# A four-stage transformer kernel on one core: row and column tiles of TensorE for the first cross attention

## What is computed

```python
x = x + tanh(g_xattn[0]) * L0_xattn(layernorm(x), ctx_1024, ...)   # stage A
x = x + tanh(g_ffn[0])   * L0_ffn(layernorm(x), ...)               # stage B
x = x + tanh(g_xattn[1]) * L1_xattn(layernorm(x), ctx_1024, ...)   # stage C
x = x + tanh(g_ffn[1])   * L1_ffn(layernorm(x), ...)               # stage D
```

```python
q = _ln((x @ Wq + bq).reshape(b, s1, H, HD), qn_w, qn_b)
k = _ln(kv[..., :HD], kn_w, kn_b)            # main; k_dca in the same way
ctx = _attn(qT, k, v)                        # softmax(q k^T / 4) v, per head
ctx_dca = _attn(qT, k_dca, v_dca)
return (ctx + ctx_dca) @ Wo + bo
```

## Time and profile before

| what | us |
|---|---|
| median of 3 runs (458.19 to 460.11) | 458.24 |
| the profiled execution, its own time | 458.89 |
| its span, first to last instruction | 457.1 |
| start to the first scores of stage A (TensorE at 30.74) | 30.7 |
| stage A from there to the first matmul of stage B (131.62) | 100.9 |
| stages B, C and D | 325.5 |

### The profile page before, as it was taken

How to read it: one execution, slowest core, us unless ns; L and a number is a source line. 1 busy time by engine, 2 the same in 40 slices (tenths; PEclk the granted TensorE clock), 3 DMA queues, 4 the chain that set the end, 5 groups by cost and what they waited for, 6 DMA issues and landing times. The chain is left out here.

```text
span 457.1 us, 8007 instructions
## 1 busy us (share of the span) xinstructions
PE 413.4 (90%) x3098; PEld 385.6 (84%) x3098; DVE 326.3 (71%) x727; ACT 206.9 (45%) x420; POOL 164.6 (36%) x199
## 2 busy tenths in 40 slices
PE   1877898987999999998989999999999999699995
PEld 1656887876889999997979899999998989599994
DVE  4787738686248696867755889889989979946642
ACT  4376347575323333243433654556456255323331
POOL 4115214242302213132222544754653553433332
PEclk9999589999899999999999999999999999989999
DMA  7201202020300110303010001001000100000000
GB/s 229 86 17 54 70 1 69 1 69 1 115 3 1 61 55 2 115 1 116 2 43 29 1 1 60 2 1 50 11 1 2 48 1 2 0 1 24 25 24 24
DMA packets 6811, 16.27 MB, mean 36 GB/s; under 512 B 1123, under 2 KB 4452, under 8 KB 6261
## 3 DMA queue, kind: packets, MB, share of 16 engines
q1 hardware_dynamic: 6772, 15.75, 10.3%
HBM read 14.70 MB, written 1.05 MB: 34 GB/s over the span
## 5 line engine op out<-in xcount | busy, mean ns | idle before, releaser
L1514 POOL TENSOR_SCALAR work<-work,lut_step,lut 128x344 f32<-128x344 int32 (+1 forms) x60 | 42.1, 713 | 55.6 <-DVE work L1441 53.7
L308 PE MATMUL ps<-wB_hi,workr 128*128 128x256 f32 x224 | 51.9, 295 | 6.1 <-POOL workr L1669 4.6
L308 PE MATMUL ps<-xT_hi,wB_hi 128*128 128x256 f32 x176 | 51.7, 293 | 0.0
L308 PE MATMUL ps<-xT_hi,wB_lo 128*128 128x256 f32 x176 | 50.1, 284 | 0.0
L308 PE MATMUL ps<-xT_lo,wB_hi 128*128 128x256 f32 x176 | 50.1, 284 | 0.0
L308 PE MATMUL ps<-wN_hi,shared_r 128*128 128x256 f32 x256 | 47.5, 280 | 1.2 <-DVE x L1428 1.2
L1107 POOL TENSOR_TENSOR workr<-work,workr 128x256 fp32r<-128x256 f32 (+1 forms) x36 | 22.9, 636 | 69.8 <-ACT workr L990 69.8
L308 PEld LDWEIGHTS ps<-wB_hi,workr 128*128 128x128 f32 x224 | 38.9, 191 | 8.1 <-POOL wB_lo L1519 3.8
L1456 DVE COPY_PREDICATED work<-work 128x1376 f32<-128x1376 int32 (+5 forms) x36 | 41.3, 1147 | 2.3
L308 PEld LDWEIGHTS ps<-wN_hi,shared_r 128*128 128x128 f32 x256 | 40.1, 188 | 1.5 <-DVE shared_r L1418 1.3
L308 PE MATMUL ps<-xT_hi,wM_hi 128*128 128x256 f32 x128 | 36.7, 287 | 3.6 <-ACT work L1282 2.2
(11 more groups left out here) (209 smaller groups left out, 1179.2 us busy)
## 6 DMA issues: line engine op xcount, KB each, us to landing
stage<-in_wC SPq DMA_DIRECT2D x4, 1280.0 KB, 5.5
stage<-in_wB SPq DMA_DIRECT2D x4, 768.0 KB, 4.3
stage<-in_idx SPq DMA_DIRECT2D x4, 536.0 KB, 3.4
stage<-in_wA SPq DMA_DIRECT2D x2, 512.0 KB, 5.4
out<-x SPq DMA_DIRECT2D x4, 256.0 KB, 2.1
x<-in_x SPq DMA_DIRECT2D x2, 256.0 KB, 4.9
x<-in_x SPq DMA_DIRECT2D x1, 512.0 KB, 6.2
ctx_n<-in_ctx_n SPq DMA_DIRECT2D x4, 128.0 KB, 2.1
```

The lines of the kernel that those rows point to most:

```text
L308: last = nc.tensor.matmul(out, l, r, start=start and i == 0, stop=stop and i == 2)
L1514: nc.gpsimd.tensor_scalar(lev[:, j, 0:n], bits[:, 0, 0:n], lut_step[:, j:j + 1], lut[:, 2 * j:2 * j + 1], ALU.mult, ALU.add).then_inc(*C[" ...
```

## The change

Scores: the keys stay undivided in `kT`; each head pair has a 32-row tile of `qx` and of `kT`, four such tiles (rows 0, 32, 64, 96) work for four banks. 32 matmuls of 64 columns take the place of 8 of 256. Values: the weight operand is now `v2`, 32 columns (two heads, of which one is zero), the moving operand 64 columns of `pT`; tiles are 64 rows by 32 columns, and the output has features in its rows, so `an`, its four copies and its turn are gone. 64 matmuls take the place of 16. The softmax halves are head pairs (banks 0 and 1, then 2 and 3), each over all four sequences, and one semaphore stands behind all the scores. The four `an` copies and `act_A_k` leave ScalarE, and `dve_A_k` has two instructions for six. `pe_A_values` waits for both halves' `pT`.

Biases: `bias_sel` adds the upper and the lower part in one matmul for two (both stand in `bias_r`, rows 0 to 63 and 64 to 127). `pe_A` is put in another order, `an_lo` is waited for between the two shifts, and the `keep_warm` counts differ: none between values and scores, 12 and 4 in the last group. `wS_lo` and the mask setup move from the start and group 0 to the end of group 2; the `sel` copies from ScalarE to GpSimd; `wS` and `sel` load beside `stage`, not into it. At the start, the lower parts of `wA` are made in three pieces, the output weights' last.

```diff
-        def pe_A_scores(pe, n, t):
+        def pe_A_scores(pe, n):
...
             for c in range(DC):
-                o = ps[:, 2 * t + c, :].rearrange("p (a b n) -> p a b n", a=PAIRS0, b=2)
-                for b in range(2):
-                    k = c * BG + 2 * t + b
-                    last = nc.tensor.matmul(o[:, :, b, :], qx[:, k].rearrange("p h n -> p (h n)"),
-                                            kx[:, k], start=b == 0, stop=False,
-                                            skip_group_check=True)
+                for b in range(BG):
+                    k = c * BG + b
+                    for p in range(PAIRS0):
+                        r = slice(32 * p, 32 * p + 32)
+                        last = nc.tensor.matmul(ps[:, p, k * S:(k + 1) * S], qx[r, k].rearrange("p h n -> p (h n)"),
+                                                kT[r, k], start=k == 0, stop=False, skip_group_check=True)
             last.then_inc(*A["scores_done"].up())
...
-        def pe_A_values(pe, g, t):
...
-            for k in range(8):
-                last = nc.tensor.matmul(ps[:, VALUES + 2 * t, k * 64:(k + 1) * 64], pT[:, t, k, :],
-                                        vz2[g % 2][:, t, k].rearrange("p b n -> p (b n)"), start=True, stop=True)
...
+            for i in range(DC * TILES):
+                for h in range(2):
+                    for p in range(PAIRS0):
+                        for b in range(2):
+                            r = slice(S * b, S * b + S)
+                            last = nc.tensor.matmul(ps[32 * p:32 * p + 32, VALUES + 2 * b, i * S:(i + 1) * S],
+                                                    v2[g % 2][r, i % TILES, i // TILES * PAIRS0 + p, h],
+                                                    pT[r, p // 2, p % 2 * 4 + i, h * S:(h + 1) * S],
+                                                    start=i == 0 and h == 0, stop=h == 1, skip_group_check=True)
+            last.then_inc(*A["pv_done"].up())
...
             if more:
                 pe_A_kv_main(pe, n, 0)
+            pe_A_shift(pe, g, 0)
+            if more:
+                pe.wait_ge(*A["an_lo"].at(g, 0))
                 pe_A_kv_last(pe, 0)
                 pe_A_kv_bias(pe, 0)
-            pe_A_shift(pe, g, 0)
-            if g:
-                pe_A_turn_out(pe, g - 1)
-            if more:
+            pe_A_shift(pe, g, 1)
+            if more:
+                pe_A_q_main(pe, n)
+                pe_A_q_bias(pe)
                 pe_A_kv_main(pe, n, 1)
-            pe_A_shift(pe, g, 1)
-            if more:
                 pe_A_kv_last(pe, 1)
                 pe_A_kv_bias(pe, 1)
...
         def pe_A_end(pe):
-            keep_warm(6, 0)
-            pe_A_turn_out(pe, GROUPS - 1)
-            keep_warm(5, 0)
+            keep_warm(8, 0)
             pe_A_out(pe, GROUPS - 1)
             keep_warm(9, 0)
```

More of the change, by code:

```diff
@@ L319, in build @@
         pT = take(TILES * 1024).rearrange("p (t k n) -> p t k n", t=TILES, n=P)
-        vz2 = [take(TILES * 8 * 2 * 32).rearrange("p (t k b n) -> p t k b n", t=TILES, k=8, b=2) for _ in range(2)]
+        v2 = [take(TILES * 8 * 2 * 32).rearrange("p (t k h n) -> p t k h n", t=TILES, k=8, h=2) for _ in range(2)]
         bias = take(NVEC + NVK)
-        vec, veck = bias[:, 0:NVEC], bias[:, NVEC:]
-        bq, bkv = vec[:, 0:D], veck
+        b_q, b_out = slice(0, D), slice(3 * D, 4 * D)
+        b_kv = slice(D, 3 * D)
         offset = take(TILES)
@@ L362, in pe_A_kv_bias @@
         def pe_A_kv_bias(pe, t):
-            for b in (bias_hi, bias_lo):
-                last = nc.tensor.matmul(kv_bank(t), ident_A, b[:, NVEC:], start=False, stop=b is bias_lo)
-            last.then_inc(*A["kv_done"].up())
+            nc.tensor.matmul(kv_bank(t), bias_sel, bias_r[:, b_kv], start=False, stop=True
+                             ).then_inc(*A["kv_done"].up())
         def rows_by_weights(to, l_hi, l_lo, r_hi, r_lo):
@@ L376, in rows_bias @@
         def rows_bias(to, cols_of):
[L377 to L380, removed]
+            return nc.tensor.matmul(ps[:, to, :].rearrange("p (t n) -> p t n", t=TILES), bias_sel,
+                                    bc_mid(bias_r[:, cols_of], TILES), start=False, stop=True,
+                                    skip_group_check=True)
         def pe_A_q_main(pe, n):
@@ L433, in act_A_v @@
         def act_A_v(act, n):
[L435 to L438, removed]
+            for h in range(2):
+                nc.scalar.copy(v2[n % 2][:, :, :, h, h * HD0:(h + 1) * HD0],
+                               ps[:, KV:KV + 2, D:2 * D].rearrange("p t (k h n) -> p t k h n", h=2, n=HD0)[:, :, :, h, :]
                                ).then_inc(*A["v_ready"].up())
@@ L491, in dve_A_scale @@
                                         ALU.mult).then_inc(*A["scaled"].up())
[L493 to L502, removed]
         def dve_A_k(dve, n):
             dve.wait_ge(*A["qT_done"].at(n, 2))
[L507 to L512, removed]
-                                            ALU.mult, ALU.add).then_inc(*A["kT_ready"].up())
+            for i, (lo, hi) in enumerate(PARTS):
+                nc.vector.tensor_scalar(kT[:, :, lo:hi], ps[:, KT, :].rearrange("p (k n) -> p k n", n=S)[:, :, lo:hi],
+                                        cols[:, 2 + 2 * i:3 + 2 * i], cols[:, 3 + 2 * i:4 + 2 * i],
+                                        ALU.mult, ALU.add).then_inc(*A["kT_ready"].up())
         def pe_A_probs(pe, g, t):
@@ L670, in pe_A @@
                 pe_A_q_bias(pe)
+                pe_A_kv_main(pe, n, 1)
+                pe_A_kv_last(pe, 1)
+                pe_A_kv_bias(pe, 1)
                 front_pe(pe, g + 2, FRONT_A)
+            else:
+                keep_warm(12, 4)
             pe_A_probs(pe, g, 0)
@@ L736, in act_A @@
                 act_A_guess(act, n)
+                act_A_v(act, n)
             act_A_probs(act, g, 1)
@@ L787, in dve_A_start @@
             dve_A_scale(dve, 0)
-            front_lower(dve, 1, FRONT_A)
+            dve.wait_ge(wA_hi_ready, 2)
+            r = slice(NWC + 2 * D, NWA)
+            nc.vector.tensor_tensor(wA_lo[:, r], stage[:, r], wA_hi[:, r].bitcast(F32),
+                                    ALU.subtract).then_inc(wA_lo_ready, 1)
             dve_A_k(dve, 0)
+            front_lower(dve, 1, OUT_A)
             dve.wait_ge(x_in, 16)
@@ L829, in pool_A_start @@
             nc.gpsimd.memset(sel.rearrange("p k n -> p (k n)").bitcast(F32), 0.0).then_inc(padded, 1)
+            pool.wait_ge(sel_in, 16)
+            pool.wait_ge(padded, 2)
+            for i, r in enumerate((0, LOWER)):
+                nc.gpsimd.tensor_copy(sel[r:r + E + 1].rearrange("p k n -> p (k n)"), sel_raw).then_inc(sel_ready, 1)
+                pool.wait_ge(sel_ready, i + 1)
+                pool.sem_inc(waited, 1)
         def pool_A(pool, g, more):
```

207 lines of the change are left out of this document (98 added, 109 removed).

## The result

| | before | changed |
|---|---|---|
| median, us | 458.22 (457.50 to 460.11, 4 runs) | 445.71 (442.15 to 448.17, 4 runs) |
| the profiled execution's span | 457.1 | 443.3 |
| first scores of stage A | 30.74 | 29.98 |
| first matmul of stage B | 131.62 | 118.42 |
| from there to the end | 325.5 | 324.9 |

The ratio is 0.9715 with a 95% interval of 0.9641 to 0.9789: 2.9% faster. Ratios here leave out executions that are over 1.5% above the fastest of the same kernel (two of four with the scores on all rows, one each with 42 warming matmuls and with these and the old values); medians and ranges are of all. The forecast was 445. All of the gain is in stage A, as forecast, and stage B begins at 118.42 where "near 118" was forecast. But the terms that make up the sum are not the ones that I had put there.

What follows compares the result with a forecast made beforehand. TensorE was taken to bound stage A, so only less TensorE work or waiting helps. Start -3.0, group 0 -8.1, steady rounds -1.2 and -0.7, last round -0.6 sum to -13.6 from 458.9, giving 445 us; range 437 to 453.

Steps and rivals of the forecast that it cites:

- the price of the tiles: Stage A scores and values per group: scores 1.9 us, values 5.0 at 39 ns a pair, together 6.9 against 6.75 before.
- the lower bound of 3.5: Scores 1.8 us plus values 1.7 a group, if tiles run fully side by side as stage C's 64-row tiles do.
- rival 1: Scores and values: tiles run fully side by side, 3.5 to 4.8 us for both, total 432 to 437; chance 0.25.
- the forecast's own sum: Stage A savings of -13.6 us, plus 4 x (price - 6.9) if tiles cost otherwise; at 3.5 it is -27.
- Rival 2: Values and scores: feeding the tiles is the bound and slower than before, total taken as 475 us; chance 0.21.
- Rival 3 (the clock): Stage A: small tiles and waits behind the scores leave TensorE at 1.2 GHz, total 455 to 461 us; chance 0.08.
- The -8.1: Group 0's round falls from 28.9 to 20.8 us, with `wS_lo` gone, a shorter wait and the clock staying up.
- The start: Before the first scores: keys take 1.0 us for 3.04 and two thirds of bias preparation goes, -3.0 us.
- The waits behind the scores: Steady round, added TensorE waits: 0.7 us for half 0's maxima, then 1.5 for `an_lo`.
- the middle of a steady round at -3.7 and +2.9: Steady round: `keep_warm` 1.24 and 2.45 us of other work go; waits of 2.9 are added, making 15.0 into 15.4.
- the last round's terms: Last group, scores to values: 10.7 us becomes 12.0 or 12.1 through later waits, less the filled wait, turn and bias matmul.

Runs made afterwards that it cites:

- the kernel without gaps: Changed kernel with the ten warming matmuls of 512 columns ahead of x's second turn made 42 of 128 columns: 435.29 us, ratio 0.9508.
- 432.35's kernel: Kernel with 42 warming matmuls plus later wait for previous output, 11 warming matmuls in group 0's wait, last group's twelve split six and six: 432.35 us, ratio 0.9431.

## Why the prediction came out right

The total was right within 0.7 us by luck: one error of 14 us was cancelled by seven smaller ones that add up to 14 the other way. By its own steps, in us, from the profiled execution (its pieces are rounded, and so a few tenths off the last row):

| step | forecast | measured | difference |
|---|---|---|---|
| scores and values, four groups at full clock | 27.6 | 13.5 | -14.1 |
| the same, more in group 0's values (half clock) and the scores behind them (pause at 705) | 0 | 1.1 | +1.1 |
| gaps at instruction chunks | none | 5.1 | +5.1 |
| first scores | 27.7 | 30.0 | +2.3 |
| between scores and values, group 0 | 13.9 | 15.8 | +1.9 |
| the same, the two steady rounds | 30.8 | 31.8 | +1.0 |
| the same, last group | 12.1 | 13.3 | +1.2 |
| behind the last values | 5.9 | 7.5 | +1.6 |
| stage B begins | 118.0 | 118.4 | |

- **The step that failed is the price of the tiles**, "Together 6.9, in effect unchanged". Measured: 1.40 + 1.94 = 3.3 a group. The scores were right (1.9). The values, put at 39 ns a pair since "feeding them should be the limit", cost 11 ns a pair. Both are at the lower bound of 3.5 that was worked out from stage C's pairs; rival 1 had the right mechanism at 0.25. With the tiles at that price the forecast's own sum gives 431; the kernel without gaps is at 435.29, and with the small edits, which the forecast didn't have, at 432.35.
- Rival 2, that feeding the tiles is slower than before, is refuted for the average: 5.5 ns an instruction. But feeding is a limit in another way that no case had: not a rate but a supply in chunks of 256, worth 5.1 us here. The supply was a term that the prediction put at nothing without a reason. The Trainium skill's page "TensorE: Matmul & The Clock Gate", section "Wait — 56ns, not 53.3ns?", gives about 62 ns per MATMUL where the sequencer decodes; the 11 ns a pair of the values are far below that, so the case that it names isn't the one of this kernel, or its figure doesn't hold for tiles. The Trainium skill's page "TensorEngine Tiling (Array Packing)", section Instruction Overhead, gives a matmul about 60 cycles; one behind the other, 128 of them would be 3.2 us by that, an estimate, and the 1.40 us don't agree.
- Rival 3 (the clock), at 0.08, was true in part: a mean of 0.83, 0.91, 0.84 and 0.82 in the rounds where 1.00 had been forecast for three. The small tiles alone are not the reason: with them the clock can stay full throughout (the trace of 432.35's kernel), and with the old values it fell for 20 us. That the waits are the reason isn't shown either; filling one of them moved nothing that could be measured.
- Group 0 was to keep its clock and lose 2.0 us with `wS_lo` gone from VectorE. TensorE's wait only shrank from 3.34 to 2.93. From the first scores on, the lower part of x is there 2.3 us earlier (13.3 us for 15.7), but TensorE has less to do and comes to the wait 1.9 earlier (10.4 for 12.3). The -8.1 became -9.2 only because the tiles were cheaper.
- The start gained 0.8 and not 3.0: TensorE waits 2.93 us for x's second turn there, which on ScalarE is queued behind v and the guess.
- The waits behind the scores (0.50 for 0.7, 1.03 for 1.5) were there, and the keys take 0.99 us for 3.04. So the middle of a steady round at -3.7 and +2.9 was nearly right: 15.6 and 16.2 us for 15.4.
- Two slips of the sum mattered little: the 15.00 us of a steady round's middle already hold the two waits that the text names beside them, and the last round's terms (10.7 - 1.3 + 1.5 + 0.7 + 0.7 - 0.6) give 11.7, not 12.0 or 12.1.

## What to carry to other kernels

Matmuls with few rows, few weight columns and few moving columns can be packed into tiles: here four 32-row tiles gave 3.6 times, and eight 64x32 tiles brought a pair of load and matmul from 109 to 11 ns, though with four times the pairs the block only went from 3.49 to 1.40 us. Once TensorE takes an instruction every few nanoseconds, look for gaps inside its blocks with no releaser: here they stood at fixed instruction numbers, behind 256 instructions that took 3.1 us or less (the fastest without a gap behind them took 3.4), and instructions added or taken away where the engine waits anyway moved them out of the fast stretch. And with less to do, TensorE waited more here and its clock was lower; so compare kernels at like granted clock before calling a difference the edit's.

## What the runs showed that I had not expected

- An instruction every 5.5 ns over 256 instructions (1.40 us), with the row and column tiles alternating in the order of the instructions.
- Gaps of 1.15 to 4.09 us ahead of instructions 705, 1217, 1473, 1729 and 2241, each 256 or a multiple from the next, in whichever matmul stands there: 256 instructions never took less than 2.8 us from border to border.
- Edits of warming matmuls alone, with the same work, moved the time from 448.92 to 435.29 us.
